# Two dequantisation scales move to GpSimd, and the hidden row's limit becomes one VectorE instruction

## The chip, the cores and the metric

The kernel runs on one core of one Trainium2 chip. The metric is the device time of one execution in microseconds, here the median of several runs. Engines are named as in the profile: PE is TensorE, DVE is VectorE, ACT is ScalarE, POOL is GpSimd, SP is SyncE, which here only issues DMAs.

## What is computed

The input x is 16 images of 512 channels and 24 x 8 positions. A channel and spatial attention (layer norm over channels, pooled gates, a 7 x 7 convolution of channel mean and maximum) is added to x. Then each position is a token of 512 numbers and goes through a feed-forward block with quantised operands:

```python
def _bitlinear(x, w):
    rms = rsqrt(maximum(mean(w * w), EPS))
    w_quant = clip(round(w * rms), -1.0, 1.0) / rms
    scale = 127.0 / maximum(max(abs(x), axis=-1, keepdims=True), EPS)
    x_quant = clip(round(x * scale), -128.0, 127.0) / scale
    return einsum('bsd,fd->bsf', x_quant, w_quant)

h = _bitlinear(layer_norm(t), w1)      # 512 -> 2048
h = gelu(h)
t = t + _bitlinear(h, w2)              # 2048 -> 512
```

PE multiplies the rounded integers, so each product has to be multiplied per token by the row's limit (the larger of the row's largest magnitude and EPS = 1e-5) times 1/(127 rms). That is the dequantisation scale. The one of the first product is called s1, that of the second s2.

## The kernel before

Two images are a pair of 384 tokens, cut into three tiles of 128 tokens; there are 8 pairs and 24 tiles, numbered n = 3 * pair + s. Tokens lie on the 128 partitions. All engines run one written-out order of steps and meet by semaphores only. In each turn of the loop `body(pair)` a pair finishes its feed-forward block while the next pair (`nxt`) is quantised and multiplied with w1, the pair after it (`att`) goes through attention, and the one after that (`fresh`) is turned into tokens. The last turns lack the later pairs. Before the loop the weights are rounded and turned, and the first pairs are started.

A tile n passes these steps:

- DVE `add_attention` (L791) writes t and its statistics; GpSimd `rstd2` (L450) forms rs2 from them in two small instructions, L434 and L435.
- DVE `centre` (L804) subtracts the mean (L810), takes the row maximum (L811), waits for rs2, and then runs four one-column instructions in a chain: lim1 (L814), rec1 (L815), s1 (L818), q1 (L820). `link` makes DVE wait for the instruction's own completion before the next. q1 releases GpSimd `round_x` (L455, L459).
- PE turns the rounded row (L1110), ACT copies it to xq, PE `ffn_in` multiplies with w1 (L1125), and ACT `gelu` (L553) reads the product with scale s1 and writes the row g of 2048 numbers.
- DVE `hidden_max` (L822) reduces each half of g to a maximum. `hidden_scale` (L828) runs four one-column instructions: lim2 (L831), s2 (L835), lim127 = lim2/127 (L836), q2 = 1/lim127 (L838). q2 releases GpSimd `round_g` (L461), which rounds the two halves of g in place (L465).
- ACT `pack_g` writes g16, SP transposes it by DMA into hq, PE `ffn_out` multiplies with w2 (L1136), and DVE `add_ffn` (L843) multiplies by s2 and adds t. PE turns the result and ACT copies it to `out_sb`.

GpSimd's order in a turn is, for s = 0, 1, 2: `rstd2` and `round_x` of tile s of the next pair, for s = 2 `normalise1` of the first tile of the fresh pair, then `round_g` of tile 3 * pair + s + 2; at the end `normalise1` of the other two tiles of the fresh pair (L440 to L442 and two L447). `normalise1` writes v1, which PE turns for the pooling (L1058), DVE takes the maxima (L740) and ACT the means.

Both g buffers and both `out_sb` buffers lie in `w1_room`, the memory of the raw w1.

Of the kernel before, what the change touches and what calls it, by code (L numbers as in the profile page):

```python
# [5 lines left out]
def metaformer_kernel(nc, x, fc1_w, fc2_w, sa_w, w1, w2, out):  # L6
# [12 lines left out]
    ALU, ACT, AX = mybir.AluOpType, mybir.ActivationFunctionType, mybir.AxisListType  # L19

    B, C, H, W = x.shape
    F = w1.shape[0]
# [3 lines left out]
    P = 128  # L26
    IMG = H * W
    TOK = 2 * IMG
    NT = TOK // P
    NC = C // P  # L30
    NF = F // P
    FB = F // 512
# [3 lines left out]
    EPS = 1e-5  # L36
# [8 lines left out]
    with ctx:  # L45
        def sb(name, shape, dt=f32):
            return ctx.enter_context(nc.sbuf_tensor(name, shape, dt))
# [4 lines left out]
        def sem(name):  # L52
            return ctx.enter_context(nc.semaphore(name))


        w1_room = sb("w1_room", [P, NF * C])
# [11 lines left out]
        w_rms = sb("w_rms", [P, 2])  # L68
        w_unit = sb("w_unit", [P, 2])
# [24 lines left out]
        t = [sb(f"t{i}", [P, NT, C]) for i in range(2)]  # L94
        cen = [sb(f"cen{i}", [P, C]) for i in range(2)]
        xq = [sb(f"xq{i}", [P, NT, NC, P], f16) for i in range(2)]
        g = [w1_room[:, i * F:(i + 1) * F] for i in range(2)]
        g16 = [w2_raw[:, 0, i * F // 2:(i + 1) * F // 2].bitcast(f16) for i in range(2)]
        hq = [sb(f"hq{i}", [P, NF, P], f16) for i in range(2)]
        res = [sb(f"res{i}", [P, C]) for i in range(2)]  # L100
        out_sb = [w1_room[:, 2 * F + i * NC * TOK:2 * F + (i + 1) * NC * TOK].rearrange("p (k t) -> p k t", k=NC)
                  for i in range(2)]
        junk = sb("junk", [P, F], bf16)
        junk_v = sb("junk_v", [P, F], bf16)
# [29 lines left out]
        lim1 = sb("lim1", [P, 1])  # L134
        rec1 = sb("rec1", [P, 1])
        q1 = [sb(f"q1_{i}", [P, 1]) for i in range(2)]
        s1 = [sb(f"s1_{i}", [P, NT]) for i in range(2)]
        amax2 = sb("amax2", [P, 2])
        lim2 = sb("lim2", [P, 1])
        lim127 = sb("lim127", [P, 1])  # L140
        q2 = [sb(f"q2_{i}", [P, 1]) for i in range(2)]
        s2 = [sb(f"s2_{i}", [P, 1]) for i in range(3)]
# [52 lines left out]
        w_turned = sem("w_turned")  # L195
# [32 lines left out]
        h_done = sem("h_done")  # L228
        g_ready = sem("g_ready")
        q2_ready = sem("q2_ready")  # L230
        g_rounded = sem("g_rounded")
        g16_ready = sem("g16_ready")
        h_turned = [[sem(f"h_turned{i}_{half}") for half in range(2)] for i in range(2)]
# [51 lines left out]
        def wait(eng, semaphore, value):  # L285

            if value > 0:
                eng.wait_ge(semaphore, value)
# [88 lines left out]
        def _(pool):  # L377
# [77 lines left out]
            def round_x(tile):  # L455

                wait(pool, q1_ready, tile.at(1, 1))
                c = cen[tile.par]
                pool.tensor_scalar(c[:, :], c[:, :], q1[tile.par][:, 0:1], MAGIC, ALU.mult, ALU.add).then_inc(cen_rounded, 1)  # L459

            def round_g(tile):  # L461
                wait(pool, q2_ready, tile.at(1, 1))
                for half in range(2):
                    part = g[tile.par][:, half * F // 2:(half + 1) * F // 2]
                    pool.tensor_scalar(part, part, q2[tile.par][:, 0:1], MAGIC, ALU.mult, ALU.add).then_inc(g_rounded, 1)  # L465

            normalise1(Pair(0), 0, 1, 2)
            weight_rms(0)
# [31 lines left out]
        def _(act):  # L500
# [51 lines left out]

            def gelu(tile, gate=None, banks=h_loop, blocks=range(FB)):  # L553

                wait(act, q1_ready, tile.at(1, 1))
                for b in blocks:
                    if b == 0 and gate:
                        gate_tokens(gate)
                    wait(act, h_done, tile.at(FB, b + 1))
                    copy(g[tile.par][:, b * 512:(b + 1) * 512], banks[b], g_ready, ACT.Gelu,  # L560
                         scale=s1[tile.pair.par][:, tile.s:tile.s + 1])
# [136 lines left out]
        def _(dve):  # L698
            class Chain:
# [5 lines left out]
                def link(self, ins):  # L705
                    self.done += 1
                    ins.then_inc(vector_step, 1)
                    self.wait()
# [5 lines left out]
                def wait(self):  # L714
                    dve.wait_ge(vector_step, self.done)
# [19 lines left out]
            def token_max(pair, k, bank):  # L735

                wait(dve, v1_turned, pair.at(NC, k + 1))
                if k == 0:
                    wait(dve, fc1_done, pair.at(1))
                dve.tensor_reduce(pooled[:, k, 0:2], front[bank][:, 0:TOK].rearrange("p (i t) -> p i t", i=2),  # L740
                                  AX.X, ALU.max).then_inc(max_ready, 1)
# [49 lines left out]
            def add_attention(tile):  # L791

                par, s = tile.pair.par, tile.s
                t_tile = t[par][:, s, :]
                wait(dve, scaled, tile.at(1, 1))
                wait(dve, xt_ready, tile.at(1, 1))
                wait(dve, res_ready, tile.at(1, 1 - 2 * NT))
                link(dve.scalar_tensor_tensor(t_tile, pv[par][:, s, :], sg[par][:, s:s + 1],  # L798
                                              xt[par][:, s, :], ALU.mult, ALU.add))
                link(dve.bn_stats(st2[:, :], t_tile))  # L800
                wait(dve, rs2_ready, tile.at(1, -1))
                dve.bn_aggr(mv2[tile.par][:, :], st2[:, :]).then_inc(stats2_ready, 1)

            def centre(tile):  # L804

                par, s = tile.pair.par, tile.s
                t_tile, c = t[par][:, s, :], cen[tile.par]
                wait(dve, stats2_ready, tile.at(1, 1))
                wait(dve, xq_turned, tile.at(1, -1))
                link(dve.tensor_scalar(c[:, :], t_tile, mv2[tile.par][:, 0:1], None, ALU.subtract))  # L810
                link(dve.tensor_reduce(amax1[:, :], c[:, :], AX.X, ALU.max, apply_absolute_value=True))  # L811
                wait(dve, rs2_ready, tile.at(1, 1))
                r = rs2[tile.par][:, 0:1]
                link(dve.tensor_scalar(lim1[:, :], amax1[:, :], r, EPS, ALU.mult, ALU.max))  # L814
                link(dve.reciprocal(rec1[:, :], lim1[:, :]))  # L815
                wait(dve, w_unit_ready, 1)
                wait(dve, g_ready, tile.at(FB, FB - NT * FB))
                link(dve.tensor_scalar(s1[par][:, s:s + 1], lim1[:, :], w_unit[:, 0:1], None, ALU.mult))  # L818
                wait(dve, cen_rounded, tile.at(1, -1))
                dve.tensor_scalar(q1[tile.par][:, :], rec1[:, :], r, 127.0, ALU.mult, ALU.mult).then_inc(q1_ready, 1)  # L820

            def hidden_max(tile, i):  # L822

                wait(dve, g_ready, tile.at(FB, (i + 1) * FB // 2))
                chain.mark(dve.tensor_reduce(amax2[:, i:i + 1], g[tile.par][:, i * F // 2:(i + 1) * F // 2], AX.X,  # L825
                                             ALU.max, apply_absolute_value=True))

            def hidden_scale(tile):  # L828

                chain.wait()  # L830
                link(dve.tensor_scalar(lim2[:, :], amax2[:, 0:1], amax2[:, 1:2], EPS, ALU.max, ALU.max))  # L831
                if tile_first(tile):
                    wait(dve, w_unit_ready, 2)
                wait(dve, res_ready, tile.at(1, -2))
                chain.mark(dve.tensor_scalar(s2[tile.third][:, :], lim2[:, :], w_unit[:, 1:2], None, ALU.mult))  # L835
                link(dve.tensor_scalar(lim127[:, :], lim2[:, :], 1.0 / 127.0, None, ALU.mult))  # L836
                wait(dve, g_rounded, tile.at(2, -2))
                dve.reciprocal(q2[tile.par][:, :], lim127[:, :]).then_inc(q2_ready, 1)  # L838

            def tile_first(tile):  # L840
                return tile.at() == 0

            def add_ffn(tile):  # L843


                wait(dve, o_done, tile.at(1, 1))
                wait(dve, q2_ready, tile.at(1, 1))
                dve.scalar_tensor_tensor(res[tile.par][:, :], ps_o[:, :], s2[tile.third][:, 0:1],  # L848
                                         t[tile.pair.par][:, tile.s, :], ALU.mult, ALU.add).then_inc(res_ready, 1)

# [18 lines left out]
            def round_weights(k, raw):  # L869

                dve.wait_ge(w_rms_ready, k + 1)
                for i in (0, 2):
                    part = quarter(k, raw, i)
                    dve.tensor_scalar(part, part, w_rms[:, k:k + 1], MAGIC, ALU.mult, ALU.add).then_inc(w_even_rounded, 1)
                link(dve.reciprocal(w_unit[:, k:k + 1], w_rms[:, k:k + 1]))
                dve.tensor_scalar(w_unit[:, k:k + 1], w_unit[:, k:k + 1], 1.0 / 127.0, None,
                                  ALU.mult).then_inc(w_unit_ready, 1)
# [70 lines left out]
            token_max(pair1, 2, 0)  # L948
            round_weights(1, w2_raw)
            add_attention(Tile(pair0, 1))  # L950
            token_max(pair1, 3, 1)
            copy_weights(1, (1,))
            hidden(pair1)
# [394 lines left out]
```

## Time and profile before

| | |
|---|---|
| time, median of 3 runs | 325.58 us (324.95 to 325.89) |
| the profiled execution | 325.85 us, of which the span from first to last instruction is 324.1 us |
| busy in the span | PE 276.8, DVE 266.0, ACT 217.5, POOL 150.0 us |
| mean granted TensorE clock | 0.975 |

Busy time is an average over stages. Times of the trace are microseconds from the start of the span unless marked ns. A number in brackets behind a row of the timeline is how long the engine had been idle, and what released it.

### The profile page before, as it was taken

The numbers are of one execution on the slowest core, as the hardware profiler recorded it, in microseconds if no ns is written. First come the engines' busy times: TensorE is split into PE (matmuls) and PEld (weight loads), VectorE is DVE, ScalarE is ACT, GpSimd is POOL, SyncE is SP. The second block draws the span as 40 slices with busy tenths as digits, with TensorE's granted clock in tenths as the row PEclk, the third lists the DMA queues.
The fourth block names the chain that finished last, engine by engine and source line by source line (L and its number), as shares of the span: only waits on it lengthen the run. The fifth ranks groups of instructions, "written<-read, shape, count | busy, mean of one in ns | idle before, by whom it ended". The sixth has DMA issues, their size and how long they took to land.

```text
span 324.1 us, 5882 instructions
## 1 busy us (share of the span) xinstructions
PE 276.8 (85%) x1834; PEld 154.8 (48%) x1834; DVE 266.0 (82%) x661; ACT 217.5 (67%) x442; POOL 150.0 (46%) x208
## 2 busy tenths in 40 slices
PE   2557669595999989998999899989998998999974
PEld 2444644553356445644564556454645453544431
DVE  0757979889699889998998899889998998899710
ACT  2286397587576976697669766976697668677731
POOL 7405355314855275437443744374437442455320
PEclk9999999878799999999999999999999999999998
DMA  4899300003065309330933094209320653083392
GB/s 130 316 384 423 109 1 2 0 0 67 1 163 67 66 7 254 68 65 2 260 68 61 4 257 70 55 13 255 73 51 17 162 68 65 1 165 68 71 218 97
DMA packets 71078, 34.20 MB, mean 106 GB/s; under 512 B 52040, under 2 KB 68424, under 8 KB 70536
## 3 DMA queue, kind: packets, MB, share of 16 engines
q1 hardware_dynamic: 69384, 32.78, 40.5%
q10 hardware_dynamic: 1664, 1.05, 1.2%
q8 instruction: 15, 0.25, 0.3%
q14 instruction: 15, 0.12, 0.1%
HBM read 14.94 MB, written 6.29 MB: 66 GB/s over the span
## 4 chain that ended last, share of the span: by engine, by line
PE 38%; DVE 22%; POOL 13%; ACT 11%; issue 10%; DMA 3%; SPq 1%; ACTq 0%; POOLq 0%; DVEq 0%
PE ps_o L1136 9%; PE ps_t L1125 7%; PE ps_h L1125 7%; POOL w_room L465 4%; POOL v L447 4%; DVE amax L825 4%; ACT w_raw L506 3%; ACT junk_p L506 3%; PE front L1048 2%; DVE pooled L740 2%; PE front L1058 2%; POOL rs L441 2%; PE small L1074 2%; PE ps_t L1167 2%; DVE t L798 2%
## 5 line engine op out<-in xcount | busy, mean ns | idle before, releaser
L1136 PE MATMUL ps_o<-w2T,hq 128*128 128x512 f16 x384 | 92.7, 380 | 1.3 <-DMA hq<-w_raw 1.3
L465 POOL TENSOR_SCALAR w_room<-w_room,q 128x1024 f32<-128x1024 f32 x48 | 59.8, 1259 | 68.9 <-DVE q L838 68.9
L825 DVE TENSOR_REDUCE amax<-w_room 128x1 f32<-128x1024 f32 x48 | 57.1, 1207 | 1.5 <-ACT w_room L506 1.5
L1125 PE MATMUL ps_h<-w1T,xq 128*128 128x512 f16 x208 | 53.9, 403 | 1.1 <-ACT xq L506 0.7
L1136 PEld LDWEIGHTS ps_o<-w2T,hq 128*128 128x128 f16 x384 | 35.4, 98 | 37.5 <-issue 3.7
L506 ACT ACTIVATE w_raw<-w_room 128x1024 f16<-128x1024 f16 x48 | 49.4, 1049 | 0.9 <-POOL w_room L465 0.9
L1125 PE MATMUL ps_t<-w1T,xq 128*128 128x512 f16 x176 | 43.3, 384 | 0.0
L506 ACT ACTIVATE w_room<-ps_h,s 128x512 f32<-128x512 f32 x52 | 35.1, 689 | 12.2 <-PE ps_h L1125 11.1
L506 ACT ACTIVATE junk_m<-front 128x192 bf16<-128x192 f32 x64 | 20.5, 329 | 24.6 <-DVE pooled L740 24.5
L506 ACT ACTIVATE w_room<-ps_t,s 128x512 f32<-128x512 f32 x44 | 30.4, 690 | 7.3 <-PE ps_t L1125 6.5
L459 POOL TENSOR_SCALAR cen<-cen,q 128x512 f32<-128x512 f32 x24 | 16.7, 695 | 35.6 <-DVE q L820 35.6
L1125 PEld LDWEIGHTS ps_h<-w1T,xq 128*128 128x128 f16 x208 | 19.5, 102 | 24.2 <-issue 4.1
L1058 PE MATMUL front<-id,v 128*128 128x128 f32 x96 | 18.3, 313 | 11.3 <-POOL v L447 7.4
L1125 PEld LDWEIGHTS ps_t<-w1T,xq 128*128 128x128 f16 x176 | 17.0, 99 | 20.9 <-issue 1.4
L848 DVE SCALAR_TENSOR_TENSOR res<-ps_o,s,t 128x512 f32<-128x512 f32 x24 | 17.8, 742 | 10.0 <-PE ps_o L1136 10.0
L798 DVE SCALAR_TENSOR_TENSOR t<-pv,sg,xt 128x512 f32<-128x512 f32 x24 | 23.0, 960 | 0.3
L1048 PE MATMUL front<-id,x_in 128*128 128x128 f32 x96 | 17.5, 320 | 6.7 <-DMA x_in<-in_x 5.8
L1058 PEld LDWEIGHTS front<-id,v 128*128 128x128 f32 x96 | 12.6, 159 | 19.0 <-POOL v L447 9.2
L727 DVE BATCH_NORM_STATS2 st<-xt 128x6 f32<-128x512 f32 x24 | 15.6, 681 | 6.9 <-ACT xt L506 6.9
L447 POOL TENSOR_SCALAR v<-xt,minus_mean,rs 128x512 f32<-128x512 f32 x24 | 19.8, 831 | 1.4
L506 ACT ACTIVATE w_room<-front 128x512 f32<-128x512 f32 x24 | 14.1, 588 | 8.6 <-PE front L1145 8.6
L740 DVE TENSOR_REDUCE pooled<-front 128x2 f32<-128x384 f32 x32 | 17.5, 547 | 2.0 <-PE front L1058 1.8
(124 smaller groups left out, 461.2 us busy)
## 6 DMA issues: line engine op xcount, KB each, us to landing
out<-w_room SPq DMA_DIRECT2D x16, 384.0 KB, 3.3
x_in<-in_x SPq DMA_DIRECT2D x14, 384.0 KB, 5.3
w_room<-in_L_ffn_w SPq DMA_DIRECT2D x4, 1024.0 KB, 8.9
w_raw<-in_L_ffn_w SPq DMA_DIRECT2D x4, 1024.0 KB, 12.0
x_in<-in_x ACTq DMA_DIRECT2D x2, 384.0 KB, 3.8
hq<-w_raw SPq DMA_TRANSPOSE x48, 3.2
fc_raw<-in_L_conv_fc_w ACTq DMA_DIRECT2D x2, 128.0 KB, 4.3
taps_rev<-in_L_conv_sa_w SPq DMA_DIRECT2D x2, 0.2 KB
```

Source lines behind the costliest of these rows:

```text
L447: pool.tensor_scalar(v1[:, s, :], xt[pair.par][:, s, :], minus_mean[:, s:s + 1], rs1[:, s:s + 1], ALU.add, ALU.mult).then_inc(normed, 1)
L459: pool.tensor_scalar(c[:, :], c[:, :], q1[tile.par][:, 0:1], MAGIC, ALU.mult, ALU.add).then_inc(cen_rounded, 1)
L465: pool.tensor_scalar(part, part, q2[tile.par][:, 0:1], MAGIC, ALU.mult, ALU.add).then_inc(g_rounded, 1)
L506: act.activation(out_ap, in_ap, func, **more).then_inc(signal, 1)
L740: dve.tensor_reduce(pooled[:, k, 0:2], front[bank][:, 0:TOK].rearrange("p (i t) -> p i t", i=2), AX.X, ALU.max).then_inc(max_ready, 1)
L798: link(dve.scalar_tensor_tensor(t_tile, pv[par][:, s, :], sg[par][:, s:s + 1], xt[par][:, s, :], ALU.mult, ALU.add))
L825: chain.mark(dve.tensor_reduce(amax2[:, i:i + 1], g[tile.par][:, i * F // 2:(i + 1) * F // 2], AX.X, ALU.max, apply_absolute_value=True))
L848: dve.scalar_tensor_tensor(res[tile.par][:, :], ps_o[:, :], s2[tile.third][:, 0:1], t[tile.pair.par][:, tile.s, :], ALU.mult, ALU.add).the ...
L1048: last = pe.transpose(front[bank][:, tile_cols(k)], x_in[tile.pair.par][:, k, tile_cols(tile.s)], id32[:, :])
L1058: last = pe.transpose(front[bank][:, tile_cols(s)], v1[:, s, tile_cols(k)], id32[:, :])
L1125: last = pe.matmul(banks[b], xq[tile.pair.par][:, tile.s, k, :], w1T[:, k, b * 512:(b + 1) * 512], start=(k == 0), stop=(k == NC - 1))
L1136: last = pe.matmul(ps_o[:, :], hq[tile.par][:, k, :], w2T[:, k, :], start=(k == 0), stop=(k == NF - 1))
```

## The change

GpSimd forms s1 behind `round_x` and s2 behind `round_g`. The gelu waits for `s1_ready`, `add_ffn` for `s2_ready`. `hidden_scale` has two instructions instead of four: lim127 = max(m0, m1)/127 and q2. The floor EPS comes from a word behind each row: the rows of g are 8 words further apart, the word behind the row holds EPS, and the maximum of the second half reads 1025 words. As lim127 is now read by GpSimd, DVE waits for s2 of the tile before. The factor 1/127 of the second weight scale goes away.

```diff
+        GSTEP = F + 8
+        g = [w1_room[:, i * GSTEP:i * GSTEP + F] for i in range(2)]
+        g_eps = [w1_room[:, i * GSTEP + F:i * GSTEP + F + 1] for i in range(2)]
...
             def round_x(tile):
...
+                if tile.at() == 0:
+                    pool.wait_ge(w_unit_ready, 1)
+                wait(pool, g_ready, tile.at(FB, FB - NT * FB))
+                pool.tensor_scalar(s1[tile.pair.par][:, tile.s:tile.s + 1], lim1[:, :], w_unit[:, 0:1], 1.0,
+                                   ALU.mult, ALU.mult).then_inc(s1_ready, 1)
             def round_g(tile):
...
+                if tile.at() == 0:
+                    pool.wait_ge(w_unit_ready, 2)
+                wait(pool, res_ready, tile.at(1, -2))
+                pool.tensor_scalar(s2[tile.third][:, :], lim127[:, :], w_unit[:, 1:2], 1.0,
+                                   ALU.mult, ALU.mult).then_inc(s2_ready, 1)
...
             def gelu(tile, gate=None, banks=h_loop, blocks=range(FB)):
-                wait(act, q1_ready, tile.at(1, 1))
+                wait(act, s1_ready, tile.at(1, 1))
...
                 link(dve.reciprocal(rec1[:, :], lim1[:, :]))
-                wait(dve, w_unit_ready, 1)
-                wait(dve, g_ready, tile.at(FB, FB - NT * FB))
-                link(dve.tensor_scalar(s1[par][:, s:s + 1], lim1[:, :], w_unit[:, 0:1], None, ALU.mult))
                 wait(dve, cen_rounded, tile.at(1, -1))
...
             def hidden_max(tile, i):
                 wait(dve, g_ready, tile.at(FB, (i + 1) * FB // 2))
-                chain.mark(dve.tensor_reduce(amax2[:, i:i + 1], g[tile.par][:, i * F // 2:(i + 1) * F // 2], AX.X,
+                if tile.at() < 2:
+                    dve.wait_ge(eps_ready, 2)
+                first = tile.par * GSTEP
+                chain.mark(dve.tensor_reduce(amax2[:, i:i + 1],
+                                             w1_room[:, first + i * F // 2:first + (i + 1) * F // 2 + i], AX.X,
                                              ALU.max, apply_absolute_value=True))
             def hidden_scale(tile):
                 chain.wait()
-                link(dve.tensor_scalar(lim2[:, :], amax2[:, 0:1], amax2[:, 1:2], EPS, ALU.max, ALU.max))
-                if tile_first(tile):
-                    wait(dve, w_unit_ready, 2)
-                wait(dve, res_ready, tile.at(1, -2))
-                chain.mark(dve.tensor_scalar(s2[tile.third][:, :], lim2[:, :], w_unit[:, 1:2], None, ALU.mult))
-                link(dve.tensor_scalar(lim127[:, :], lim2[:, :], 1.0 / 127.0, None, ALU.mult))
+                wait(dve, s2_ready, tile.at())
+                link(dve.tensor_scalar(lim127[:, :], amax2[:, 0:1], amax2[:, 1:2], 1.0 / 127.0, ALU.max, ALU.mult))
                 wait(dve, g_rounded, tile.at(2, -2))
                 dve.reciprocal(q2[tile.par][:, :], lim127[:, :]).then_inc(q2_ready, 1)
...
             def add_ffn(tile):
                 wait(dve, o_done, tile.at(1, 1))
-                wait(dve, q2_ready, tile.at(1, 1))
+                wait(dve, s2_ready, tile.at(1, 1))
...
             def round_weights(k, raw):
...
+                if k == 1:
+                    dve.reciprocal(w_unit[:, k:k + 1], w_rms[:, k:k + 1]).then_inc(w_unit_ready, 1)
+                    return
...
             add_attention(Tile(pair0, 1))
+            dve.wait_ge(w_turned, 8)
+            for i in range(2):
+                dve.memset(g_eps[i], EPS).then_inc(eps_ready, 1)
             token_max(pair1, 3, 1)
```

## Rows read from the trace of the kernel before

**Rows 1.** Windows of one loop turn: length, busy us of each engine, clock, DMA.

```profile
121.78:154.43 32.65, 30.58 (x211) 16.71 (x209) 29.79 (x78) 23.73 (x52) 16.83 (x24) 1.00 0.42 98
...
219.68:252.31 32.63, 30.60 (x211) 16.68 (x209) 29.76 (x79) 23.74 (x52) 16.83 (x24) 1.00 0.42 98
```

**Rows 2.** The chain that ended last, three pieces of one loop turn.

```profile
157.48 0.52 PE front L1058 x3
...
178.03 0.29 DVE stat_split L776
...
187.06 0.55 DVE pooled L740
```

**Rows 3.** Timeline of the last third of that turn: start, us, engine, line.

```profile
178.84 0.21 DVE L831 TENSOR_SCALAR lim<-amax 128x1 f32<-128x1 f32 x1
...
179.08 0.21 DVE L835 TENSOR_SCALAR s<-lim,w_unit 128x1 f32<-128x1 f32 x1
...
179.39 0.17 DVE L838 RECIPROCAL q<-lim 128x1 f32<-128x1 f32 x1
...
179.65 2.22 POOL L465 TENSOR_SCALAR w_room<-w_room,q 128x1024 f32<-128x1024 f32 x2 [1.37 <-DVE q L838]
...
181.93 0.76 DVE L798 SCALAR_TENSOR_TENSOR t<-pv,sg,xt 128x512 f32<-128x512 f32 x1
181.96 0.19 POOL L440 TENSOR_SCALAR ve<-mv 128x2 f32<-128x2 f32 x1
...
182.23 1.01 POOL L441 TENSOR_TENSOR rs<-ve,half_pow 128x2 f32<-128x2 f32 x1
...
183.53 1.68 POOL L447 TENSOR_SCALAR v<-xt,minus_mean,rs 128x512 f32<-128x512 f32 x2
183.67 0.91 DVE L810 TENSOR_SCALAR cen<-t,mv 128x512 f32<-128x512 f32 x1
...
186.23 0.21 DVE L814 TENSOR_SCALAR lim<-amax,rs 128x1 f32<-128x1 f32 x1 [0.93 <-POOL rs L435]
...
186.68 0.21 DVE L818 TENSOR_SCALAR s<-lim,w_unit 128x1 f32<-128x1 f32 x1
186.93 0.21 DVE L820 TENSOR_SCALAR q<-rec,rs 128x1 f32<-128x1 f32 x1
...
190.11 0.52 PE L1058 MATMUL front<-id,v 128*128 128x128 f32 x3 [0.29 <-ACT junk_m L506]
```

**Rows 4.** Four lines of the kernel: duration in ns, least, median, most.

```profile
L434 POOL TENSOR_SCALAR ve<-mv x24: 192/201/482, 43.2 to 296.9; 128x1 f32<-128x1 f32 x24
...
L459 POOL TENSOR_SCALAR cen<-cen,q x24: 690/695/702, 45.2 to 299.1; 128x512 f32<-128x512 f32 x24
...
L447 POOL TENSOR_SCALAR v<-xt,minus_mean,rs x24: 759/767/1130, 12.0 to 249.5; 128x512 f32<-128x512 f32 x24
...
L917 DVE MEMSET sharp_bias<- x1: 59/59/59, 1.0 to 1.0; 128x1 f32 x1
```

**Rows 5.** Who waited for whom: us in total, times, longest us.

```profile
POOL w_room L465 <- DVE q L838: 68.9, 24, 6.9
```

**Rows 6.** The same chain, its first and last passes through L831 and L814.

```profile
71.35 0.14 DVE lim L831
...
75.99 0.22 DVE lim L814
...
285.41 0.23 DVE lim L831
...
290.14 0.22 DVE lim L814
```

**Rows 7.** Timeline near the end: one instruction of DVE, one of PE.

```profile
265.48 1.13 DVE L798 SCALAR_TENSOR_TENSOR t<-pv,sg,xt 128x512 f32<-128x512 f32 x1
...
291.90 0.40 PE L1110 MATMUL front<-id,cen 128*128 128x128 f16 x4 [0.19 <-POOL cen L459]
```

**Rows 8.** Window of four microseconds before the loop, granted clock 0.50.

```profile
80.00:84.00 4.00, 4.00 (x50) 2.07 (x51) 3.84 (x13) 1.49 (x3) 3.26 (x4) 0.50 0.00 0
```

More of the change, by code:

```diff
@@ L96, in metaformer_kernel @@
         xq = [sb(f"xq{i}", [P, NT, NC, P], f16) for i in range(2)]
-        g = [w1_room[:, i * F:(i + 1) * F] for i in range(2)]
+        GSTEP = F + 8
+        g = [w1_room[:, i * GSTEP:i * GSTEP + F] for i in range(2)]
+        g_eps = [w1_room[:, i * GSTEP + F:i * GSTEP + F + 1] for i in range(2)]
         g16 = [w2_raw[:, 0, i * F // 2:(i + 1) * F // 2].bitcast(f16) for i in range(2)]
@@ L100, in metaformer_kernel @@
         res = [sb(f"res{i}", [P, C]) for i in range(2)]
-        out_sb = [w1_room[:, 2 * F + i * NC * TOK:2 * F + (i + 1) * NC * TOK].rearrange("p (k t) -> p k t", k=NC)
+        out_sb = [w1_room[:, 2 * GSTEP + i * NC * TOK:2 * GSTEP + (i + 1) * NC * TOK].rearrange("p (k t) -> p k t", k=NC)
                   for i in range(2)]
@@ L138, in metaformer_kernel @@
         amax2 = sb("amax2", [P, 2])
-        lim2 = sb("lim2", [P, 1])
         lim127 = sb("lim127", [P, 1])
@@ L230, in metaformer_kernel @@
         q2_ready = sem("q2_ready")
+        s1_ready = sem("s1_ready")
+        s2_ready = sem("s2_ready")
+        eps_ready = sem("eps_ready")
         g_rounded = sem("g_rounded")
@@ L830, in hidden_scale @@
                 chain.wait()
-                link(dve.tensor_scalar(lim2[:, :], amax2[:, 0:1], amax2[:, 1:2], EPS, ALU.max, ALU.max))
-                if tile_first(tile):
-                    wait(dve, w_unit_ready, 2)
-                wait(dve, res_ready, tile.at(1, -2))
-                chain.mark(dve.tensor_scalar(s2[tile.third][:, :], lim2[:, :], w_unit[:, 1:2], None, ALU.mult))
-                link(dve.tensor_scalar(lim127[:, :], lim2[:, :], 1.0 / 127.0, None, ALU.mult))
+                wait(dve, s2_ready, tile.at())
+                link(dve.tensor_scalar(lim127[:, :], amax2[:, 0:1], amax2[:, 1:2], 1.0 / 127.0, ALU.max, ALU.mult))
                 wait(dve, g_rounded, tile.at(2, -2))
                 dve.reciprocal(q2[tile.par][:, :], lim127[:, :]).then_inc(q2_ready, 1)
-            def tile_first(tile):
-                return tile.at() == 0
             def add_ffn(tile):
                 wait(dve, o_done, tile.at(1, 1))
-                wait(dve, q2_ready, tile.at(1, 1))
+                wait(dve, s2_ready, tile.at(1, 1))
                 dve.scalar_tensor_tensor(res[tile.par][:, :], ps_o[:, :], s2[tile.third][:, 0:1],
```

## The prediction

> **What bounds the kernel now.** I first looked for a period, with windows cut at the same instruction of each loop turn. Five turns in a row, from 89.14 to 252.31 us, are all 32.6 us long [rows 1]. In one such turn PE is busy for 30.6 us and DVE for 29.8. So neither is idle for long, and neither is full: about 2 us of waiting for PE and nearly 3 for DVE. The busy shares alone can't say what an instruction less on DVE is worth.
>
> So I read the chain that ended last, through one turn [rows 2]. It has four sections. From 187.06 (in the turn shown, from 154.43) it is DVE with its maxima, then PE without a gap from 157.48 for some 15 us, then ACT packing g and summing channels until 178.03, and then DVE, GpSimd and DVE again until 187.06. Only the last section holds anything that the change touches, and it holds both places: `hidden_scale` at 178.84, behind it GpSimd from 179.65, and `centre` at 186.23 [rows 3]. In that section DVE itself is early. It sat idle for 0.93 us before L814 until GpSimd's rs2 came. GpSimd's queue from 179.65 to rs2 is `round_g`, `normalise1`, `rstd2`, and nothing in it has room.
>
> Then I counted how often the whole chain goes through the two places. It passes L831 8 times, first at 71.35 and last at 285.41, and L814 9 times, first at 75.99 and last at 290.14 [rows 6]: twice each before the five turns, once each in every turn, and the rest behind them. The other 16 and 15 executions lie where PE or ACT sets the pace.
>
> **What goes from VectorE.** In `hidden_scale`, the instruction behind the link of L831 starts at 179.08 and q2 at 179.39 [rows 3]. With lim127 in L831's place (the same operands, one operation exchanged, so I keep its 0.21 us) q2 can start at 179.08. That is 0.31 us a tile. In `centre`, s1 starts at 186.68 and q1 at 186.93, so q1 comes 0.25 us earlier. On the chain this is 8 x 0.31 + 9 x 0.25 = 4.73 us. Over all 24 tiles it would be 13.4 us, but most of that only lengthens DVE's waits for PE, ACT and GpSimd.
>
> **What GpSimd gains: s1.** It stands behind `round_x`. Every one of the 24 `round_g` waited for q2 [rows 5], so s1 sits in an idle stretch and costs the chain nothing. In the turn shown GpSimd was idle for 1.37 us before 179.65, behind a `normalise1` of the fresh pair. The gelu that needs s1 has in between the turn on PE, the copy on ACT and the first product, together more than 1.5 us. If that cover were gone, s1 would cost what s2 costs.
>
> **What GpSimd gains: s2.** This is the dear one. It stands behind `round_g`, and queued behind it are `normalise1` and `rstd2`, for whose rs2 DVE is already idle. There is no s2 on GpSimd in this trace. The nearest instruction is L434, one column with two constants: 0.192 us at least, 0.201 median, 0.482 at most [rows 4]. A column as operand instead of a constant adds to it: `round_x` with one takes 0.695, v1 of the same 512 elements with two takes 0.767, so 0.07 each. That makes 0.26. The gap from the end of `round_g` at 181.87 to the next start at 181.96 is 0.09 [rows 3], and a part of it may come a second time. Against it, rs at 182.23 and the second v1 now lose time beside DVE's L798 and L810, and a later start can lose less there: the two v1 take 1.68 where twice the median is 1.53. I take 0.31 for all of it. The bounds are 0.19 (the shortest one-column instruction, its gap hidden) and 0.57 (the longest L434 and a whole gap). Below nothing it can't go, since the order behind it is unchanged.
>
> In the six passes where GpSimd itself is on the chain this counts in full. In the first (71.35) and the last (285.41) pass DVE reached L814 within 0.1 us of rs2, so I count it there too: 8 x 0.31 = 2.48 us given back.
>
> The Trainium skill speaks against this edit. Its page "SBUF — State Buffer", section "Who interferes with whom", says that a DVE instruction with two SBUF inputs and a GpSimd instruction that reads SBUF exclude each other, and that the second one is blocked until the first ends. The trace agrees in part: ve began 0.03 us behind L798, which has such inputs, and took its least, 0.19 us, while rs behind it took 1.01.
>
> **The other edits.** The new wait of `hidden_scale` for s2 of the tile before: that s2 ends about 3 us behind its q2, and the next `hidden_scale` comes 7 us or more later in the loop (5 us at the very end), so it is met. Were it not, `hidden_max` and `add_ffn` would queue behind it. The wait of s2 for `res_ready` (tile n - 3) is always met, for DVE runs that `add_ffn` before the `hidden_scale` that releases this `round_g`. `add_ffn` needs s2 only after the packing, the transposes and w2. The 1025th word costs a nanosecond on 1.2 us. Two one-column memsets of 59 ns [rows 4] stand in DVE's order ahead of the last maximum of pair 1, on the chain: 0.12 us. The dropped multiplication by 1/127 in `round_weights` precedes a t (L798) that waits for GpSimd's large rounding beside it, so it gives nothing; without that cover it would give 0.1.
>
> **The end.** Two corrections. At 265.48 a t (L798) takes 1.13 us where it takes 0.76 elsewhere [rows 7, 3]; it stands beside the first half of a `round_g` that begins with q2, while DVE here starts when PE is done. An earlier q2 ends that half sooner, and I take 0.3 off. Later PE works on without a gap up to 291.90, where it waited for only 0.19 us [rows 7], so not all of what the last passes of the two places save can come through: I give back 0.3.
>
> **Sum.** 4.73 - 2.48 - 0.12 + 0.3 - 0.3 = 2.1 us. The profiled execution took 325.85 us (324.1 of span and 1.75 around it), so 323.7. It stood 0.27 above the median of the runs; against the median the forecast is 323.4 us. In one turn that is 0.31 + 0.25 - 0.31 = 0.25 us: 32.63 becomes 32.4.
>
> **Rivals.**
>
> *s2 costs next to nothing* because later starts of rs and v1 lose less beside L798 and L810 than they do now. For it: the 0.15 us that v1 loses. Against it: v1 would now start at about 183.8, behind L810 (183.67) and not ahead of it. Then 4.7 us come through, 0.8 of which the bounds of s2 still allow against: 320.9 to 321.5. Chance 0.09.
>
> *The gain stays under what can be told from no change.* Either s2 costs its upper bound, so that 4.73 - 8 x 0.57 = 0.2 us are left, or PE takes over. PE's wait at 190.11 was 0.29 us [rows 3], and PE's own work before it hangs on v1, which becomes no earlier, since the 0.31 of q2 and the 0.31 of s2 cancel. If that slack is smaller than it looks, a turn gains 0.1 and the whole 0.8 or so. 324.7 to 325.5. Chance 0.18.
>
> *The other side: s2 falls into L798 and waits for its end.* In the turn shown s2 would be due at 181.96, where ve was, just behind L798 (181.93 to 182.69). If it is held there, ve and all behind it go back by 182.69 - 181.96 = 0.73 us and more than the DVE saves: 8 x 0.73 - 4.73 + 0.12 = 1.2 us, 326.8. It decides from 4.73 / 8 = 0.59 us a pass on. Against it stands that ve in the same place was not held, and that rs now bears such a hold itself, which would then go. Chance 0.08. The skill's rule named above is this rival taken at its word.
>
> *The clock.* In 80 to 84 us PE ran at a granted clock of 0.50, the 1.2 GHz level [rows 8], after a stretch in which it had mostly waited for DVE. Steps before that stretch move by some tenths. One more stretch of this length where PE is on the chain costs 2 us or more: about 325.5 to 327. Nothing in the rows makes it likely. Chance 0.05, all counted as slower.
>
> **How the numbers follow.** 0.60 for the forecast, with the rivals' 0.09, 0.18, 0.08 and 0.05. About 0.3% (1 us) is what a measurement of this kernel can tell from no change. Faster: 0.60 + 0.09 = 0.69; same 0.18; slower 0.13. With s2 at its bounds the forecast's own range is 4.61 - 8 x 0.57 = 0.05 to 4.61 - 8 x 0.19 = 3.1 us of gain. I let the range reach to the near edge of the first rival, 320.9, and beyond no change to 326.0. That leaves out the far side of the slower cases.
>
> **What the profile after will show.** Right: turns of 32.4 us; q2 starting 0.25 us behind lim127; in `centre` three starts where there were four; an s2 of 0.26 us between `round_g` and ve; DVE still idle before L814 in each turn, now for some 0.93 + 0.3 us; DVE busy for about 13 us less in the whole span and its waits longer. Wrong: if s2 or the ve behind it shows 0.4 us or more, the GpSimd section was under-priced; if L814 no longer waits for rs2, it was over-priced; if turns are unchanged and PE's wait at the place of 190.11 is gone, PE has taken over; if a further stretch of clock 0.50 appears, it is the clock.

## The result, and the profile after

| | before | after |
|---|---|---|
| median of 6 runs each | 325.42 us | 322.77 us |
| lowest and highest | 324.95 to 325.91 | 321.82 to 323.44 |
| ratio, 95% interval | | 0.9915 (0.9899 to 0.9932) |
| profiled execution, span | 325.85, 324.1 | 323.44, 321.7 |

The changed kernel is 2.65 us faster. In the profiled executions the difference is 2.41 us. The forecast was 323.4 us. One execution of `eps_later` and one of `s2_deferred_2` (both below) took 901 and 1436 us, with PE busy for 98% and 99% of the span, for a cause that nothing here shows; all medians and ratios leave them out.

The first part of the page of the kernel after, busy time and its share of the span:

```profile
PE 276.9 (86%) x1834; PEld 155.9 (48%) x1834; DVE 251.6 (78%) x590; ACT 217.7 (68%) x442; POOL 160.9 (50%) x256
```

DVE lost 14.4 us of busy time and the span 2.4. Most of what was removed lay where DVE waits anyway.

The windows of loop turns of the kernel after, columns as in [rows 1], cut at another instruction:

```profile
124.92:157.20 32.28, 30.37 (x211) 16.76 (x209) 27.73 (x69) 23.80 (x52) 18.30 (x30) 1.00 0.42 99
...
189.48:221.95 32.47, 30.36 (x210) 16.76 (x209) 27.72 (x69) 23.81 (x52) 18.30 (x30) 1.00 0.43 101
```

A turn fell from 32.63 to 32.28 us; the last two of the five are 32.5, for a reason given below. The timeline of the kernel after, in the stretch that answers to [rows 3]:

```profile
177.23 0.17 DVE L790 CAST stat_split<-ch_stat 128x6 bf16<-128x6 f32 x1 [1.03 <-ACT junk_p L520]
...
177.93 0.21 DVE L847 TENSOR_SCALAR lim<-amax 128x1 f32<-128x1 f32 x1
...
178.18 0.16 DVE L849 RECIPROCAL q<-lim 128x1 f32<-128x1 f32 x1
...
178.44 2.21 POOL L474 TENSOR_SCALAR w_room<-w_room,q 128x1024 f32<-128x1024 f32 x2 [1.39 <-DVE q L849]
...
180.63 0.27 POOL L478 TENSOR_SCALAR s<-lim,w_unit 128x1 f32<-128x1 f32 x1
...
180.71 0.75 DVE L812 SCALAR_TENSOR_TENSOR t<-pv,sg,xt 128x512 f32<-128x512 f32 x1
...
180.98 0.54 POOL L444 TENSOR_SCALAR ve<-mv 128x2 f32<-128x2 f32 x1
...
181.60 0.71 POOL L445 TENSOR_TENSOR rs<-ve,half_pow 128x2 f32<-128x2 f32 x1
...
182.44 0.49 DVE L824 TENSOR_SCALAR cen<-t,mv 128x512 f32<-128x512 f32 x1
...
182.60 1.72 POOL L451 TENSOR_SCALAR v<-xt,minus_mean,rs 128x512 f32<-128x512 f32 x2
...
185.33 0.21 DVE L828 TENSOR_SCALAR lim<-amax,rs 128x1 f32<-128x1 f32 x1 [1.68 <-POOL rs L439]
185.58 0.17 DVE L829 RECIPROCAL rec<-lim 128x1 f32<-128x1 f32 x1
185.78 0.21 DVE L831 TENSOR_SCALAR q<-rec,rs 128x1 f32<-128x1 f32 x1
```

Read it against [rows 3]. From the start of lim to that of q2 it was 0.55 us and is 0.25: 0.30 less, where 0.31 was worked out. s2 takes 0.27 and starts with no gap. ve then takes 0.54 instead of 0.19: it began at 180.98, in the middle of DVE's t (180.71 to 181.46), and ended 0.06 behind it. And rs takes 0.71 instead of 1.01, now that no t stands beside it. From q2 to L814 it was 6.84 us and is 7.15: 0.31 more, the sum that was forecast, but made of other parts.

The chain that ended last, in the kernel after, where this section ends (the first line is the turn of v1 on PE, `turn_v1`, the last the first product):

```profile
184.38 0.55 PE front L1072 x3
...
188.96 0.52 PE front L1072 x3
189.48 1.78 PE ps_h L1139 x8
```

Before, the chain went from here through rs2, `centre` and the maxima on DVE, and PE waited 0.29 us at the last `turn_v1` [rows 3]. Now that wait is gone and the chain runs on PE from v1 on. From the end of v1 to the first product it was 5.41 us and is 5.15. So the 0.25 us that s1 left on DVE came through, and used up nearly all of the 0.29 us that PE had waited.

### The profile page after: what moved, and what is told of

The parts are those of the page before. It is cut to its first block, busy times and chain, and to the rows that moved or that the text cites. A ratio compares the mean times of both kernels' runs of the same rounds, so it can differ in the third digit from the quotient of the medians.

```text
span 321.7 us, 5840 instructions
## 1 busy us (share of the span) xinstructions
PE 276.9 (86%) x1834; PEld 155.9 (48%) x1834; DVE 251.6 (78%) x590; ACT 217.7 (68%) x442; POOL 160.9 (50%) x256
## 4 chain that ended last, share of the span: by engine, by line
PE 50%; DVE 12%; POOL 12%; ACT 12%; issue 9%; DMA 3%; SPq 1%; ACTq 0%; POOLq 0%; DVEq 0%
PE ps_o L1150 16%; PE ps_h L1139 9%; PE ps_t L1139 8%; POOL w_room L474 4%; POOL v L451 4%; PE front L1072 4%; ACT w_raw L520 3%; ACT junk_p L520 3%; PE front L1062 3%; PE ps_t L1181 2%; PE small L1088 2%; ACT junk L520 2%; DVE w_room L882 2%; POOL rs L445 2%; PE front L1159 1%
## 5 line engine op out<-in xcount | busy, mean ns | idle before, releaser
L839 DVE TENSOR_REDUCE amax<-w_room 128x1 f32<-128x1024 f32 (+1 forms) x48 | 57.1, 1208 | 2.2 <-ACT w_room L520 2.2
L1139 PE MATMUL ps_h<-w1T,xq 128*128 128x512 f16 x208 | 54.6, 408 | 0.9 <-ACT xq L520 0.9
L812 DVE SCALAR_TENSOR_TENSOR t<-pv,sg,xt 128x512 f32<-128x512 f32 x24 | 21.2, 885 | 0.3
```

Of the source, the lines that this page charges most:

```text
L839: chain.mark(dve.tensor_reduce(amax2[:, i:i + 1], w1_room[:, first + i * F // 2:first + (i + 1) * F // 2 + i], AX.X, ALU.max, apply_absolu ...
L1139: last = pe.matmul(banks[b], xq[tile.pair.par][:, tile.s, k, :], w1T[:, k, b * 512:(b + 1) * 512], start=(k == 0), stop=(k == NC - 1))
```

## The experiments

Turns are taken from the starts of one instruction, DVE's first cast in `split_stats` (L776 before), which comes once a turn.

| kernel | median us | ratio to before, 95% interval | turn us |
|---|---|---|---|
| before | 325.4 | | 32.63 |
| after_again | 322.64 | 0.9916 (0.9894 to 0.9939) | 32.28 |
| s2_on_dve | 321.37 | 0.9872 (0.9850 to 0.9893) | 31.96 |
| s2_deferred | 320.82 | 0.9869 (0.9846 to 0.9891) | 31.95 |
| three_memsets | 322.65 | 0.9921 (0.9904 to 0.9937) | 32.27 |
| s1_on_dve | 324.48 | 0.9971 (0.9958 to 0.9984) | 32.52 |
| limit_only | 322.21 | 0.9903 (0.9885 to 0.9920) | 32.19 |
| rows_apart | 325.47 | 1.0000 (0.9989 to 1.0011) | 32.60 |
| eps_later | 320.77 | 0.9858 (0.9843 to 0.9873) | – |
| s2_deferred_2 | 320.69 | 0.9857 (0.9835 to 0.9879) | – |
| eps_later_2 | 321.34 | 0.9876 (0.9857 to 0.9894) | 31.97 |

**s2_on_dve: s2 back on VectorE, but behind q2.**

```diff
                 dve.reciprocal(q2[tile.par][:, :], lim127[:, :]).then_inc(q2_ready, 1)
...
+                wait(dve, res_ready, tile.at(1, -2))
+                dve.tensor_scalar(s2[tile.third][:, :], lim127[:, :], w_unit[:, 1:2], None,
+                                  ALU.mult).then_inc(s2_ready, 1)
```

The same instruction of GpSimd is taken out of `round_g`.

> s2 goes back to VectorE, but behind q2 and not ahead of it; s1 stays on GpSimd. Theory (s2 costs the GpSimd section about 0.3 us in each pass): from q2 to the end of v1 falls from 6.15 to 5.83 us, a turn from 32.28 to 31.97, and the kernel stands 1.3 to 2.2 us below the changed one, near 321. Rival 1 (PE took over in the turn and sets 32.3 whatever GpSimd does): turns stay at 32.2 to 32.3. Rival 2 (VectorE bounds): its 0.13 to 0.21 us more a tile lengthens the turn, and the time is that of the changed kernel or above.

A turn is 31.96 us, 0.32 less than after, and the median 1.3 us below after_again; the two profiled executions, 323.44 and 321.63 us, differ by 1.8. s2 behind `round_g` did cost 0.32 us a turn, and neither PE nor DVE stood in the way when it went.

**s2_deferred: s2 stays on GpSimd, behind the next round_x.**

```diff
                         round_x(Tile(pair.plus(1), s))
+                        scale_2(Tile(pair, s + 1))
```

`scale_2` holds the wait and the instruction that stood at the end of `round_g`; the tiles at either end are placed by hand in the same way.

> s2 stays on GpSimd but moves behind round_x of the next tile, where GpSimd waits for q2. Theory: as with s2 on VectorE a turn is 31.97 us, and as neither engine pays, the time is at or slightly below that one: 320.5 to 321.3. Rival (what counts is one instruction more in GpSimd's queue, wherever it stands): as the changed kernel, 322.5 to 323.

The timeline of this kernel in the same section of a turn, GpSimd and DVE's t:

```profile
176.03 2.21 POOL L481 TENSOR_SCALAR w_room<-w_room,q 128x1024 f32<-128x1024 f32 x2 [1.39 <-DVE q L855]
...
178.30 0.76 DVE L818 SCALAR_TENSOR_TENSOR t<-pv,sg,xt 128x512 f32<-128x512 f32 x1
178.32 0.19 POOL L444 TENSOR_SCALAR ve<-mv 128x2 f32<-128x2 f32 x1
178.60 1.02 POOL L445 TENSOR_TENSOR rs<-ve,half_pow 128x2 f32<-128x2 f32 x1
...
179.90 1.67 POOL L451 TENSOR_SCALAR v<-xt,minus_mean,rs 128x512 f32<-128x512 f32 x2
```

ve starts 0.02 us behind t again and is back at 0.19, rs is at 1.02, as before the change, and the section is 0.3 us shorter. A turn is 31.95 us. The instruction is the same on the same engine: its place made the price, not its being there.

**three_memsets: more work on GpSimd behind s2.**

```diff
+        spare = sb("spare", [P, 72])
...
                                   ALU.mult, ALU.mult).then_inc(s2_ready, 1)
+                for i in range(3):
+                    pool.memset(spare[:, 3 * tile.at() + i:3 * tile.at() + i + 1], 1.0)
```

> The changed kernel with three one-column memsets on GpSimd behind each s2, some 0.3 us of work that reads no SBUF. Theory A (ve is held until L812, VectorE's t with two SBUF inputs, ends, so work that fits ahead of that end is free): ve ends where it did, 0.04 to 0.1 us behind t, the turn stays within 0.1 us of 32.3, and the time grows by under 0.8 us, from the passes in which t is elsewhere. Rival B (GpSimd's section is a plain sum): a turn grows by 0.3 us and the time by 2 to 2.5 us.

The timeline of this kernel:

```profile
179.71 0.26 POOL L479 TENSOR_SCALAR s<-lim,w_unit 128x1 f32<-128x1 f32 x1
...
179.79 0.75 DVE L815 SCALAR_TENSOR_TENSOR t<-pv,sg,xt 128x512 f32<-128x512 f32 x1
...
179.91 0.15 POOL L482 MEMSET spare<- 128x1 f32 x3
...
180.13 0.46 POOL L445 TENSOR_SCALAR ve<-mv 128x2 f32<-128x2 f32 x1
...
180.68 0.71 POOL L446 TENSOR_TENSOR rs<-ve,half_pow 128x2 f32<-128x2 f32 x1
```

The memsets took 0.15 us together, not the 0.3 that I had reckoned, so this is a weaker test in the time than planned: ve starts only 0.07 us later behind s2 than without them. The trace has to decide it. ve starts 0.34 us behind t instead of 0.27 and ends at 180.59, 0.05 behind t's end at 180.54, where it ended 0.06 behind it without them. A turn is 32.27 against 32.28, and the median 322.65 against 322.64. So ve waits here for the end of t, and the little that was put ahead of that end was free. The Trainium skill says this of such pairs of instructions ("SBUF — State Buffer", "Who interferes with whom"), and here the trace agrees; it also exempts a GpSimd instruction that only writes, as a memset does, and these began and ended inside t.

**s1_on_dve: s1 back in its old place, the rest as changed.**

```diff
                 link(dve.reciprocal(rec1[:, :], lim1[:, :]))
...
+                link(dve.tensor_scalar(s1[par][:, s:s + 1], lim1[:, :], w_unit[:, 0:1], None, ALU.mult))
```

The gelu waits for `q1_ready` again, and `round_x` has no s1.

> The changed kernel with s1 back on VectorE in its old place; s2 stays on GpSimd. Theory (a turn is the GpSimd section and then VectorE's centre and maxima): the 0.25 us of s1 come back in every turn, 32.28 becomes 32.5 to 32.6, and the time 324.3 to 325.0. Rival (PE had already taken over in the turn of the changed kernel, so that s1 gave nothing there): turns stay at 32.3 to 32.4 and the time within 1 us of 322.7.

A turn is 32.52, 0.24 more than after, and the median 324.48, 1.8 us more. The rival falls: in the changed kernel PE is on the chain, but moving s1 did pay.

**limit_only: the limit alone.** This is s2_on_dve with s1 on VectorE as well, so that GpSimd has nothing new.

> Only the limit is changed: lim127 in one instruction, floor word behind each row, s2 on VectorE behind q2; s1 on VectorE in its old place, nothing new on GpSimd. Theory: 0.31 us in each of 8 passes of the chain, so a turn of 32.2 to 32.3 and 322.8 to 323.4, about what the whole change gives. Rival (the removed instructions lay where VectorE waits anyway): 324.5 or more.

322.21 us and a turn of 32.19: 0.44 less than before, where q2's 0.31 alone would give 32.32. The time lies 0.6 us below the expectation. It can't be told from that of the whole change (ratios 0.9903 and 0.9915, with intervals that overlap): the merged limit, with s2 behind q2 on VectorE, gives all of the gain, and moving the two scales to GpSimd adds nothing to it. In steps from turn to turn it is limit -0.44, s1 -0.23 (32.19 to 31.96), s2 behind `round_g` +0.32 (31.96 to 32.28). Taken in the other order, with s1_on_dve between, s2 is +0.33 (32.19 to 32.52) and s1 -0.24 (32.52 to 32.28). So the two parts add up and don't depend on each other.

The 0.13 us beyond q2 are found ahead of it. The kernel before, its timeline:

```profile
177.52 0.77 POOL L447 TENSOR_SCALAR v<-xt,minus_mean,rs 128x512 f32<-128x512 f32 x1
...
178.03 0.28 DVE L776 CAST stat_split<-ch_stat 128x6 bf16<-128x6 f32 x1 [0.59 <-ACT junk_p L506]
```

The first cast of `split_stats`, which is on the chain [rows 2], took 0.28 us and ended 0.02 behind GpSimd's v1. In the kernel after, v1 is done before the cast begins (at 177.23, above), and the cast takes 0.17:

```profile
176.29 0.76 POOL L451 TENSOR_SCALAR v<-xt,minus_mean,rs 128x512 f32<-128x512 f32 x1
```

limit_only has v1 at 176.51 to 177.27, ahead of its cast at 177.35, which takes 0.17 too. That is 0.1 of the 0.13. s1_on_dve has both cases in one execution: in four of its turns the cast takes 0.17, and in the one in which v1 is still running it ends 0.03 behind v1. v1 runs there from 210.48 to 211.24, and DVE's timeline has

```profile
210.92 0.35 DVE L785 CAST stat_split<-ch_stat 128x6 bf16<-128x6 f32 x1 [0.54 <-ACT junk_p L515]
```

Why v1 moved is argued only: DVE has one instruction less a tile in limit_only, three less in the changed kernel, and may deliver the statistics for this v1 earlier against ACT, which sets the cast's start.

**rows_apart: only the addresses.** `GSTEP = F + 8` and the places that use it, in the kernel before.

> The kernel before with nothing but the rows of g and the output buffers 8 words further apart. Both theories expect no effect of the addresses: ratio 1.000, within 0.2%. If it is off by more, part of the measured gain is one of the layout and not of the instructions.

Ratio 1.000. The layout gives nothing and costs nothing.

**after_again, after_look_1, after_look_2: where the spread comes from.**

> The changed kernel once more. Its profile before had a stretch at granted clock 0.50 from 61.0 to 71.3 us, 3.4 us longer than in the kernel before, and its six times lay in two clusters (321.8 to 322.3 and 323.2 to 323.4). If the clock stretches make the clusters, a profile of the lower cluster has a shorter or differently placed stretch before 92 us, and the five loop turns are 32.3 to 32.5 us all the same. If the turns make them, the turns differ. Median 322.2 to 323.3.

> The changed kernel, one look, to find a profile of the lower cluster of its times (321.7 to 322.3; both profiles so far are of the upper one, 323.1 to 323.8). Theory: the clusters are made before 92 us by where the stretches at clock 0.50 fall; five turns of 32.28, 32.28, 32.28, 32.5, 32.5 in either cluster, and the first cast of stat_split of pair 1 (79.5 and 79.7 us so far) earlier by the difference in time. Rival: the clusters come from the turns or from the end, and that cast is at 79.5 again.

> The changed kernel, a second look, with the same expectations as the first: if the time is near 322, the cast of stat_split of pair 1 is near 78; if near 323.5, it is near 79.6; the turns are the same in both.

The last two executions were 322.12 and 323.69 us, one of each cluster. Here are windows of four microseconds: first the kernel before, then the changed kernel (323.44 us), then after_look_1. The granted clock is the third number from the end.

```profile
68.00:72.00 4.00, 3.81 (x23) 1.37 (x20) 3.19 (x11) 3.43 (x7) 0.00 (x0) 0.91 0.00 0
```

```profile
68.00:72.00 4.00, 4.00 (x19) 1.58 (x17) 2.83 (x8) 2.80 (x5) 0.18 (x1) 0.50 0.00 0
```

```profile
68.00:72.00 4.00, 3.71 (x24) 1.48 (x22) 3.55 (x11) 3.87 (x7) 0.55 (x1) 1.00 0.00 0
```

In the execution of 323.44 us PE ran at the 1.2 GHz level from about 62 to 72 us. In that of 322.12 us it was back at 2.4 GHz before 68. At the place where the chain of the kernel before passes L831 at 71.35 [rows 6], that of the 323.44 us execution is on PE:

```profile
70.32 1.71 PE ps_h L1139 x4
```

The first cast of pair 1 shows what that costs. The kernel before, the changed kernel, and after_look_1, each from its timeline:

```profile
79.08 0.16 DVE L776 CAST stat_split<-ch_stat 128x6 bf16<-128x6 f32 x1
```

```profile
79.66 0.17 DVE L790 CAST stat_split<-ch_stat 128x6 bf16<-128x6 f32 x1
```

```profile
78.22 0.17 DVE L790 CAST stat_split<-ch_stat 128x6 bf16<-128x6 f32 x1
```

It is at 79.48 in both after_again (323.39) and after_look_2 (323.69). So the executions of the upper cluster are 1.3 to 1.4 us behind that of the lower one at this point, and 1.3 to 1.6 in the time, with turns alike. The theory holds as far as one trace of the lower cluster can show it. Twenty-three runs of the kernel before spread over 324.86 to 326.44 without such a gap; why the changed one falls in two clusters is open. A difference of a microsecond between medians of five or six runs can come from this alone, which is why the turns count for more here.

**eps_later, s2_deferred_2, eps_later_2: the two memsets moved, starting from s2_deferred.**

```diff
-            dve.wait_ge(w_turned, 8)
-            for i in range(2):
-                dve.memset(g_eps[i], EPS).then_inc(eps_ready, 1)
             token_max(pair1, 3, 1)
             copy_weights(1, (1,))
+            dve.wait_ge(w_turned, 8)
+            for i in range(2):
+                dve.memset(g_eps[i], EPS).then_inc(eps_ready, 1)
```

> The kernel with s2 behind the next round_x, and the two memsets of the floor words moved behind the weight copies of VectorE, where it waits 0.45 us for PE. Theory (the memsets stand on the chain ahead of the last maximum of pair 1): steps behind 62 us come 0.1 to 0.15 us sooner, 0.1 us in the time, at the edge of what can be measured. Rival (clock stretches before 92 us decide): the two kernels differ by their stretches, up to 1 us either way, with turns alike at 31.95 us.

> The kernel with s2 behind the next round_x once more, for its median beside the one with the later memsets on the same chip: 320.3 to 321.3, ratio to the kernel before 0.984 to 0.988.

> The later memsets once more, since the profile of the first run was of an execution disturbed as a whole. Theory: 0.1 us below s2_deferred_2 and turns of 31.95 us; a difference under 0.3 us between medians says nothing, and the trace then decides: the last maximum of pair 1 starts 0.1 us or so sooner behind the t ahead of it. Rival: it starts at the same distance, since the memsets lie beside it.

The medians are 320.77 and 321.34 with the move, 320.82 and 320.69 without: no gain. In the traces the last maximum starts 0.88 us behind the end of t in the changed kernel and 0.87 in eps_later_2, and the weight copy behind the maximum 1.35 and 1.31. The rival is right: the memsets lay beside the maximum, and cost 0.04 us at most.

## Why the prediction was right, step by step

**What bounds the kernel.** Right. The section of the chain behind `split_stats` was the only one in a turn that moved: from the first product to the next cast it is 20.03 us before (190.63 to 210.66) and 20.02 after (189.48 to 209.50).

**Counting passes.** It held for the turns. Between the first products of the first and sixth turn the kernel before took 163.17 us and the changed one 161.82: 1.35 less, where 5 x 0.25 = 1.25 was forecast. Inside it, q2 gave 0.30 and s1 0.25 in each turn, as said, and the cast another 0.1, which I hadn't seen. Against that, two of the turns lost 0.2 to a stall (below).

**s2.** The sum was right by luck, 0.31 forecast and 0.31 measured from q2 to L814, for its parts were not. s2 itself was 0.27 as reckoned from the operands. But the gap that I added didn't come, ve lost 0.35 behind t, and rs got 0.30 back. I had named the cancelling as a possibility and not worked it through: t's place was in the rows, and it would have shown that ve, not s2, falls into it. My own sign for an under-priced s2, a ve of 0.4 us or more, appeared (0.54) and meant nothing by itself.

**The rivals.** "s2 costs next to nothing": no. "PE takes over": half. It did come onto the chain in each turn, but just where s1's saving ended, so it took nothing away. "s2 held until the end of t": s2 was not held; it started 0.08 us ahead of t. ve was, and the price stayed at 0.3 since rs had paid for it before. (The times of the first rival don't fit together: 320.9 plus the 0.8 is 321.7, not 321.5. Nothing hangs on it.) The clock: it came, in another form. No further stretch appeared, but the one before 72 us, which in the kernel before ends within 68 to 72, ran to the end of that window. A chance of 0.05 for the clock was too low. The longer stretch cost the profiled execution some 1.4 us at 79 us, against the execution of 322.12 us. It also took the first pass of L831 off the chain, on which the chain of the 322.12 us execution has it, at 71.03. In the sum it hid: from the start to the first turn's product only 0.06 us were gained, where 2 x 0.56 - 2 x 0.31 - 0.12 = 0.38 was forecast, and the lower cluster gained over a microsecond more.

**The end.** Under-priced. From 255.88 the kernel before took 68.22 us, the changed one from 254.47 67.23: 0.99 less, where 0.31 + 2 x 0.25 - 0.31 + 0.3 - 0.3 = 0.5 was forecast. The t in question went from 1.13 [rows 7] to 0.80 as forecast. The kernel after, the chain:

```profile
264.07 0.80 DVE t L812
```

Another 0.38 us come from the pass through `centre` just behind it. The chain of the kernel before doesn't name this pass, so I hadn't counted it, but DVE runs it there. The kernel before, its timeline and further on its chain:

```profile
270.33 0.21 DVE L818 TENSOR_SCALAR s<-lim,w_unit 128x1 f32<-128x1 f32 x1 [0.30 <-DVE rec L815]
```

```profile
276.56 1.05 PE small L1101 x42
```

The chain of the kernel after:

```profile
274.43 1.21 PE small L1115 x42
```

From lim1 to q1 it was 0.96 us and is 0.45: 0.25 of that is s1, and 0.26 a stall of the kind that the last section describes, which the kernel before had here. At the end of t the changed kernel was 1.75 us ahead, at this step of PE it is 2.13. From 274.43 to 294.26 its chain then stays on PE: PE has taken over. On this stretch, which holds the last pass of L831 and the last two of L814, the gain grows by 0.24 us, where 0.31 + 2 x 0.25 - 0.31 - 0.3 = 0.2 was forecast.

**The memsets.** Forecast 0.12, measured 0.04 at most. **DVE's wait before L814.** 1.68 us instead of the forecast 1.2: L810 fell from 0.91 to 0.49, for v1 now starts 0.16 behind its start and not 0.14 ahead of it (in s2_deferred, with v1 0.13 ahead again, it takes 0.91).

So the start came out 0.3 us worse than forecast (the clock), the turns 0.1 and the end 0.5 better: 2.1 forecast, 2.4 in the profiled executions, 2.65 between the medians. What the turns do was forecast by its mechanism. That the total is so near is in part luck: misses at the start and at the end, neither foreseen, partly cancel.

## What to carry to other kernels

An instruction taken off a busy engine is worth what the chain's passes through it are worth, here 17 of 48. One given to an idle engine costs nothing only where that engine waits: s2 behind `round_g` gave back 0.32 us a turn, and the same instruction behind the next `round_x` gave back none, 320.7 and 320.8 us against 322.7. Price each part of a change by itself: here one merged instruction, with s2 one place further back on VectorE, would have done as much as the whole change. Before adding a small instruction to GpSimd's queue, lay VectorE's instructions with two SBUF inputs beside it and ask which one behind it will now fall into them.

## What the runs showed of the hardware

- A one-column multiplication on GpSimd with one column as operand takes 0.26 to 0.27 us, with two constants 0.19. s2, whose wait was met, followed `round_g` without a gap; ve came 0.08 us behind s2, and what makes that difference isn't shown.
- By the starts that the profile gives, ve began 0.03 us behind DVE's t in the kernel before, and 0.02 us behind it in s2_deferred, and took 0.19 us; beginning 0.27 or 0.34 us behind it, it was held until t's end plus 0.05. So a short instruction that starts almost together with t gets through. The Trainium skill ("SBUF — State Buffer", "Who interferes with whom") says that the second to issue is blocked in full; in the first of these cases the measurement differs, and it decides.
- A DVE cast of 128x6 numbers that started while GpSimd's v1 was running took 0.27 to 0.35 us and ended 0.02 to 0.03 us behind v1 (kernel before, s1_on_dve); with v1 done it took 0.17.
- Single DVE instructions start 0.24 to 0.30 us after a predecessor that is done, where others wait 0.04, at the same place in each trace of one kernel (four of the changed one). In the changed kernel and in s2_deferred, from the timelines:

```profile
210.66 0.16 DVE L849 RECIPROCAL q<-lim 128x1 f32<-128x1 f32 x1 [0.24 <-DVE lim L847]
```

```profile
207.92 0.16 DVE L855 RECIPROCAL q<-lim 128x1 f32<-128x1 f32 x1 [0.24 <-DVE lim L853]
```

Both lie on the chain and lengthen that turn by 0.2 us (32.48 and 32.15). The changed kernel has a second one in its last full turn, at q1 (250.77), and the kernel before and rows_apart one at s1, behind the turns (270.33 and 269.97). In s2_on_dve no turn has one, and in limit_only the only one (0.22, at 125.30) lengthens none. What makes the stall is open.
